# A state scan on VectorE: one multiplication of 1024 columns in place of two of 512

## The reference

```python
# d_inner 256 = 2 halves of 128, d_state 16, L 256, batch 4
def step(state, inp):
    d, b, c, u = inp
    dA = jnp.exp(d[..., None] * A)
    state = state * dA + (d * u)[..., None] * b[:, None, :]
    y = jnp.einsum('bdn,bn->bd', state, c)
    return (state, y)
_, ys = jax.lax.scan(step, state0, (dt_t, B_t, C_t, u_t))
y = ys + D * x;  y = y * silu(z)
```

## Time and profile before

| | |
|---|---|
| median of 3 runs | 593.02 us (589.87 to 594.47) |
| profiled execution, its own time | 595.68 us |
| its span | 593.4 us |
| TensorE matmul busy | 483.5 us, 81% |
| VectorE busy | 472.9 us, 80% |
| ScalarE busy | 363.0 us, 61% |
| GpSimd busy | 280.7 us, 47% |
| mean granted TensorE clock | 0.930 |

### The profile page before, as it was taken

The page is one execution under the profiler, slowest core; times in us unless marked ns, Lnnn a source line. Parts: engine busy times, 40 slices in busy tenths (PEclk is TensorE's granted clock), DMA queues, the critical chain, the costliest instruction groups (busy, mean ns, idle before and its releaser), DMA issues.

```text
span 593.4 us, 10199 instructions
## 1 busy us (share of the span) xinstructions
PE 483.5 (81%) x3040; PEld 360.9 (61%) x3050; DVE 472.9 (80%) x1246; ACT 363.0 (61%) x830; POOL 280.7 (47%) x262
## 2 busy tenths in 40 slices
PE   6817777767778879898989999998799988998823
PEld 3302222222357757576779899997689977997602
DVE  4899999999875537897666765896898969875886
ACT  2785555536227745464767676678665796778543
POOL 3119777879210444561068548732786234333111
PEclk9957999989869989899999999999999999999856
DMA  5939300001003589998242103400135000000000
GB/s 157 224 72 335 97 0 1 1 1 35 1 9 114 193 235 290 282 284 236 83 159 64 28 8 73 64 2 2 36 56 72 1 2 2 19 2 0 1 18 18
DMA packets 45624, 48.60 MB, mean 82 GB/s; under 512 B 5660, under 2 KB 42118, under 8 KB 45574
## 3 DMA queue, kind: packets, MB, share of 16 engines
q1 hardware_dynamic: 41734, 36.46, 22.6%
q0 software_dynamic: 3840, 11.54, 8.6%
HBM read 41.43 MB, written 6.56 MB: 81 GB/s over the span
## 4 chain that ended last, share of the span: by engine, by line
PE 33%; DVE 26%; issue 22%; ACT 8%; POOL 8%; DMA 1%; DVEq 1%; SPq 0%; POOLq 0%; ACTq 0%; another core or an unknown queue 0%
DVE hst L1786 7%; PE ps L1539 5%; PE ps L1478 4%; PE ps L1479 4%; PE ps L1480 4%; PE ps L1528 3%; PE ps L1395 2%; POOL dbu L524 2%; DVE hc L1795 2%; POOL G L603 2%; POOL pn L619 2%; PE ps L1292 1%; PE ps L1432 1%; PE ps L1196 1%; PE ps L1380 1%
## 5 line engine op out<-in xcount | busy, mean ns | idle before, releaser
L619 POOL TENSOR_TENSOR pn<-pr,pinv 128x512 f32<-128x512 f32 x64 | 67.6, 1059 | 88.3 <-DVE pinv L2194 87.9
L524 POOL TENSOR_TENSOR dbu<-du,brow 128x512 f32<-128x512 f32 x64 | 81.5, 1285 | 41.4 <-DVE du L1779 23.1
L1196 PE MATMUL ps<-hc,ident 128*128 128x512 f32 x128 | 75.7, 683 | 28.9 <-DVE hc L1795 27.4
L1786 DVE TENSOR_TENSOR_SCAN hst<-ps,dbu 128x512 f32<-128x512 f32 x64 | 77.4, 1210 | 0.2 <-POOL dbu L524 0.2
L762 ACT ACTIVATE ps<-dtv,amat 128x510 f32<-128x510 f32 x64 | 44.1, 690 | 50.9 <-DVE hst L1786 50.1
L938 ACT ACTIVATE pr<-ebuf,smin 128x256 f32<-128x256 f32 x128 | 63.7, 502 | 13.0 <-DVE smin L2185 6.6
L1539 PE MATMUL ps<-pT,cS 128*128 128x256 f32 x256 | 67.2, 385 | 0.0
L581 POOL DMA_INDIRECT G<-token_rows,idx_x x32 | 39.9, 1246 | 52.1 <-DVE ebuf L2039 24.0
L1196 PEld LDWEIGHTS ps<-hc,ident 128*128 128x128 f32 x128 | 21.0, 202 | 69.6 <-DVE hc L1795 66.9
L603 POOL DMA_INDIRECT G<-expert_out,idx_g x48 | 51.1, 1064 | 11.6 <-issue 10.4
L2185 DVE CUSTOM_DVE_ANT_0 ebuf<-ps,mbias 128x256 f32<-128x256 f32 x128 | 48.9, 419 | 6.2 <-issue 6.0
(11 more groups left out here) (372 smaller groups left out, 1364.8 us busy)
## 6 DMA issues: line engine op xcount, KB each, us to landing
wdn<-in_L_ffn_wd SPq DMA_DIRECT2D x15, 384.0 KB
wgu<-in_L_ffn_wg SPq DMA_DIRECT2D x14, 384.0 KB
wgu<-in_L_ffn_wu SPq DMA_DIRECT2D x14, 384.0 KB
expert_out<-xn SPq DMA_DIRECT2D x11, 256.0 KB
wq<-in_L_xattn_Wq SPq DMA_DIRECT2D x2, 1024.0 KB, 9.2
wo<-in_L_xattn_Wo SPq DMA_DIRECT2D x1, 2048.0 KB, 15.6
wo<-in_L_ffn_w SPq DMA_DIRECT2D x2, 1024.0 KB, 6.9
expert_out<-pexp SPq DMA_DIRECT2D x5, 256.0 KB
```

Source lines behind the costliest of these rows:

```text
L524: nc.gpsimd.tensor_tensor(dbu[:, j, :], du[:, j % 2, 512 * hb:512 * hb + 512], brow[:, j // 2, :], ALU.mult).then_inc(pool_dbu, 1)
L619: nc.gpsimd.tensor_tensor(pn[:, h % 2], pr[:, h % 2], pinv[:, h % 2, :].unsqueeze(2).to_broadcast([P, 2, L]), ALU.mult)\
L1196: pe.matmul(bank(2 + j % 2), ident[:], hc[:, j % 2, :], start=(isinstance(m, int) and m + k == 0), stop=(isinstance(m, int) and m + k == N ...
L1786: V.tensor_tensor_scan(hst[:, j, :], bank(j % 2), dbu[:, j, :], 0.0, ALU.mult, ALU.add)\
```

## The change

VectorE multiplies the states of both inner halves by their C row in one operation of 1024 columns, with the bank of the row broadcast over the halves. The product buffer now holds two pairs: `hc` is one, the tile `wqT`, which isn't in use yet, the other. `hc_ready` counts pairs. A pair's product is taken after both its scans, so the order for four is scan 0, pair 1 of the last group, scan 1, scan 2, pair 0, scan 3. TensorE waits once for a pair and then makes both additions. Before `sum_up(0)`, `add_scan` and `lower_logits` the last product in VectorE's order is now a pair; ahead of `sum_up(1)` the pair with both halves comes behind `choose(0)` and `shares(0)`.

```diff
+        products = (hc[:], wqT[:].rearrange("p a b l -> p a (b l)"))
...
-                for j in (2 * k, 2 * k + 1):
-                    i = 32 * hb + 4 * m + j
-                    pe.wait_ge(hc_ready, i + 1)
-                    pe.matmul(bank(2 + j % 2), ident[:], hc[:, j % 2, :], start=(isinstance(m, int) and m + k == 0),
+                pe.wait_ge(hc_ready, 16 * hb + 2 * m + k + 1)
+                for d in range(2):
+                    pe.matmul(bank(2 + d), ident[:], products[k][:, d, :], start=(isinstance(m, int) and m + k == 0),
                               stop=(isinstance(m, int) and m + k == NS // 2)).then_inc(y_added, 1)
...
-                wait_count(dve, hc_ready, i - 3)
+                wait_count(dve, hc_ready, 16 * hb + 2 * m + j // 2 - 1)
...
-            def read_out(hb, m, j):
+            def read_out(hb, m, k):
 
-                i = 32 * hb + 4 * m + j
-                dve.wait_ge(scanned, i + 1)
-                dve.wait_ge(c_spread, 16 * hb + 2 * m + j // 2 + 1)
-                wait_count(dve, y_added, i - 1)
-                V.tensor_tensor(hc[:, j % 2, :], hst[:, j, :], bank(6 + j // 2), ALU.mult).then_inc(hc_ready, 1)
+                i = 32 * hb + 4 * m + 2 * k
+                dve.wait_ge(scanned, i + 2)
+                dve.wait_ge(c_spread, 16 * hb + 2 * m + k + 1)
+                wait_count(dve, y_added, i - 2)
+                V.tensor_tensor(products[k], hst[:, 2 * k:2 * k + 2, :],
+                                bank(6 + k).unsqueeze(1).to_broadcast([P, 2, 512]), ALU.mult).then_inc(hc_ready, 1)
 
             def scan_four(hb, m, first):
-                for j in range(4):
-                    scan(hb, m, j)
-                    if j:
-                        read_out(hb, m, j - 1)
-                    elif not first:
-                        read_out(hb, m - 1, 3)
+                scan(hb, m, 0)
+                if not first:
+                    read_out(hb, m - 1, 1)
+                scan(hb, m, 1)
+                scan(hb, m, 2)
+                read_out(hb, m, 0)
+                scan(hb, m, 3)
...
-                for j in (2 * k, 2 * k + 1):
-                    scan(1, m, j)
-                    if j:
-                        read_out(1, m, j - 1)
-                    elif m:
-                        read_out(1, m - 1, 3)
-                    else:
-                        read_out(0, NS // 2 - 1, 3)
+                scan(1, m, 2 * k)
+                if k:
+                    read_out(1, m, 0)
+                elif m:
+                    read_out(1, m - 1, 1)
+                else:
+                    read_out(0, NS // 2 - 1, 1)
+                scan(1, m, 2 * k + 1)
                 if n == 0:
                     sum_up(0)
...
-            read_out(1, NS // 2 - 1, 3)
+            read_out(1, NS // 2 - 1, 1)
             sum_up(1)
```

## The result

The changed kernel takes 599.69 us (median of 6 runs, 598.64 to 602.26) against 591.15 us for the kernel before on the same chips (6 runs, 589.86 to 594.47). The ratio is 1.014, 95% interval 1.011 to 1.017: slower by 8.5 us. The profiled execution took 599.31 us with a span of 597.0. The one before took 595.68 us, more than any of its six other runs, so these two alone would say +3.6 us. Comparisons inside the scan stage are therefore made between the traces, and those of the whole kernel between the medians. What lies behind the stage can't be compared between single traces: that part of the program is the same in all nine, and from the last L1810 or its counterpart to the end of the span it took between 419.8 and 428.1 us.

The account below looks back on a forecast made before the run. The prediction took VectorE to bound the scan stage. Its terms, -1.4 + 4.6 + 1.1 + 1.6 + 1.3 = +7.2 us, carried whole onto the median of 593.02 us, gave 600.2 us, with a range of 593.5 to 605.

Parts of the forecast that it names:

- The saving: Steady scan stage: a long product's slot of 1.12 us replaces 1.16, 0.045 us a pair, -1.4 us over 31 pairs.
- both doubts: Steady scan stage: successive scans might not overlap, +2.6 us; the PSUM broadcast might cost 0.04 us an operation, leaving no saving.
- L1820 twice and L1839: Turned outputs and logits of half 0: each existing VectorE wait for TensorE grows by 1.54 us, +4.6 us.
- L1812 after the first half: First half's sums: later products cost 1.54 us less 0.44 us of cover, a wait of +1.1 us.
- The end of the stage: Last sums: the path from last multiplication becomes 4.86 us with TensorE at 1.2 GHz, +1.6 us; at 2.4 GHz +0.2.
- The start: First scans: a decay behind a B row copy behind a late spread, +1.2 us, and the third scan's decay, +0.1.
- Carried whole: Behind the scan stage: nothing swallows the delay, so all +7.2 us reach the kernel's time.
- grouping simply pays: Rival, whole kernel: late products hidden or swallowed, only the saving left, 589 to 592 us; chance 0.06 for 587 to 592.
- the third: Rival, scan stage: long product no faster than two short, -1.4 us lost, 601.6 us; inside the forecast's range, no separate chance.
- The clock rival: Second L1818: TensorE at 1.2 GHz after idling, +2.0 us; with non-overlapping scans 602 to 605 us; clock or scans chance 0.15.

Follow-up runs that it names:

- The order alone: Changed kernel with its order kept, but each pair multiplied in two operations of 512 columns that signal separately; 595.38 us, ratio 1.0064 to the kernel before.
- the late rows: Changed kernel with ScalarE's copy of a B row put one decay later in its queue; 595.75 us, ratio 1.0077 to the kernel before.
- TensorE kept busy: Changed kernel with 14 and 17 matmuls that nobody reads added at two places where TensorE sat idle; 599.77 us, ratio 1.0128 to the kernel before.
- the kernel before with a delay: Kernel before plus six chained, unread VectorE operations of 1024 columns ahead of the scan stage's last product; 599.48 us, ratio 1.0129.
- the kernel with halves: Changed kernel with the nine of 32 pairs next to a wait multiplied in single halves, in the earlier order; 589.72 us, ratio 0.9985 to the kernel before.
- the waits further on and the B rows late: Changed kernel with readers of TensorE's results one step later, B row copies one decay later, last pair in halves; 590.07 us, ratio 0.9938 to the kernel before.

## Why the prediction was right

Slower, at 600.2 us forecast and 599.69 measured, and for the reason given: products arrive later at places where VectorE then waits. That the two times lie 0.5 us apart is luck. The forecast added 7.2 us to a median of 593.02 from three runs; with six runs the kernel before has 591.15, and the growth is 8.5 us (6.5 to 10.0 by the interval). The firmer comparison is the stage: in the profiled executions it grew by 7.0 us, where 7.2 were forecast. By the prediction's own steps:

- **The saving.** Forecast -1.4 us; measured 31 x 0.065 = -2.0. The pitch of four scans fell from 6.85 to 6.72 us where 6.75 was forecast: the long product's slot is 1.11, not 1.12, and two scans on end have a pitch of 1.12. Scans overlap on end and the broadcast of a PSUM bank costs nothing over the copy in SBUF; both doubts fell on the good side. By the figure for PSUM of the Trainium skill ("Perfetto Trace Analysis", Optimizing Scalar/DVE Operations), 125 ns, it would have been an estimated 4.0 us. A removed operation gave 0.065 us here, about half of that; the same sentence of the Trainium skill has about 60 ns for SBUF, and these operations read one operand from each.
- **L1820 twice and L1839.** Forecast +4.6 us, with waits of 2.0, 2.0 and 3.0; measured 1.8, 1.8 and 2.9, so +4.2. The longer product was sized right (0.54 us), the second addition a little too high: the forecast took 0.96 us from the earlier trace rows, the distance from the start of the first addition to that of the spread, and the second one adds 0.87. The order alone showed the two parts apart.
- **L1812 after the first half.** Forecast +1.1; measured a wait of 0.94 us where there was none:

```profile
101.80 1.98 PE L1196 MATMUL ps<-wqT,ident 128*128 128x512 f32 x4 [0.94 <-DVE wqT L1795]
...
103.82 1.40 DVE L1812 SCALAR_TENSOR_TENSOR u<-u,dskip,ps 128x512 f32<-128x512 f32 x2 [0.94 <-PE ps L1196]
```

- **The end of the stage.** This term was mis-sized: +1.6 us forecast at 1.2 GHz, +0.1 measured. The timeline and the stretch (length, busy PE, PEld, DVE, ACT, POOL, granted clock, DMA share, GB/s) show 1.00 where the earlier trace rows had 0.50:

```profile
170.88 1.21 DVE L1795 TENSOR_TENSOR wqT<-hst,ps 128x1024 f32<-128x1024 f32 x1
...
172.14 1.98 PE L1196 MATMUL ps<-wqT,ident 128*128 128x512 f32 x4 [1.16 <-DVE wqT L1795]
...
174.17 1.41 DVE L1812 SCALAR_TENSOR_TENSOR u<-u,dskip,ps 128x512 f32<-128x512 f32 x2 [2.08 <-PE ps L1196]
```

```profile
172.00:174.00 2.00, 1.86 (x6) 0.81 (x7) 0.09 (x1) 0.00 (x0) 0.00 (x0) 1.00 0.22 57
```

  The path is 3.29 us; the prediction had 3.39 for 2.4 GHz and 4.86 for 1.2, and took the second because "TensorE is no busier ahead of it than before". That premise failed. The late pairs kept TensorE at work until 1.16 us before these additions, against 1.99 us in the earlier trace rows. The clock wasn't kept up throughout, though: it had fallen behind the logits and had only just come back:

```profile
164.03 3.78 PE L1196 MATMUL ps<-wqT,ident 128*128 128x512 f32 x4 [3.22 <-DVE wqT L1795]
```

```profile
168.00:170.00 2.00, 1.98 (x3) 0.94 (x3) 1.93 (x14) 0.00 (x0) 0.00 (x0) 0.50 0.00 0
170.00:172.00 2.00, 0.99 (x2) 0.07 (x1) 1.93 (x5) 0.00 (x0) 0.00 (x0) 0.95 0.04 9
```

  Before, it was 0.50 from 160 to 162 us, 0.98 in the next two and 0.50 again at the last additions. So both kernels had a fall after the logits and a return; a second fall came only before. Whether the length of the idle time decides that was not tried.
- **The start.** Forecast +1.2 for a scan that waits for ScalarE and +0.1 for the third scan; measured 1.42 and 0.0:

```profile
54.52 0.60 ACT L771 ACTIVATE brow<-ps 128x512 f32<-128x512 f32 x1 [2.74 <-PE ps L1179]
...
55.73 1.22 DVE L1786 TENSOR_TENSOR_SCAN hst<-ps,dbu 128x512 f32<-128x512 f32 x1 [1.42 <-ACT ps L763]
```

  The copy waits for the spread and the decay behind the copy, as worked out; the late rows took the wait away.
- **Not in the sum.** Two more waits for ScalarE, 0.39 us at 112.35 and 1.20 us at 137.69, each behind a fall of the clock (0.50 from 110 to 112 us, after TensorE had idled 3.40 us, and 0.50 from 130 to 136):

```profile
132.06 3.78 PE L1196 MATMUL ps<-wqT,ident 128*128 128x512 f32 x4 [5.17 <-DVE wqT L1795]
...
136.48 0.60 ACT L771 ACTIVATE brow<-ps 128x512 f32<-128x512 f32 x1 [2.62 <-PE ps L1179]
...
137.69 1.22 DVE L1786 TENSOR_TENSOR_SCAN hst<-ps,dbu 128x512 f32<-128x512 f32 x1 [1.20 <-ACT ps L763]
```

  TensorE idles 5.17 us behind the waits, its additions then take 3.78 us instead of 1.98, the spread behind them is late, and ScalarE's copy and decay with it. The prediction had named the new idle time after L1810 and after the first L1818, but priced the clock only at the second L1818; there it fell in one of the traces. The path on which a slow TensorE reaches VectorE, through ScalarE's queue, it had worked out for the start of the stage alone. TensorE kept busy removes the two, and so do the late rows. By size this omission (+1.6) made up for the end of the stage (-1.5); that the total came so close is luck in that part.

Measured, the terms are -2.0 + 4.2 + 0.9 + 0.1 + 1.4 + 1.6 = +6.2 us; the first scan started 0.1 us later, and four waits that are new each cost the 0.08 us by which neighbours otherwise overlap, +0.3. 0.4 us of the 7.0 stay unassigned.

**Carried whole.** The forecast's last step is supported by the kernel before with a delay (7.5 us in, 7.5 out). In the two traces alone it could be doubted: the first expert product comes 5.4 us later and the end 3.6. But from the last sums to the end the trace before has 426.2 us, the changed one 422.8, and the kernel with halves, which ends its stage earlier than either, 421.8. So that part varies by itself and doesn't follow the stage's end, and the medians differ by 8.5.

**The rivals.** That grouping simply pays is refuted for this placing; with the waits further on and the B rows late it holds, for 1.8 us. The long product is faster than two short ones, so the third is refuted. The clock rival is real, but in the changed kernel's profile it cost 1.6 us at other places than the one named.

The Trainium skill ("Perfetto Trace Analysis", Optimizing Scalar/DVE Operations) also says that where ScalarE or VectorE isn't saturated but makes others wait, breaking an instruction up may let work end sooner. Here VectorE is the saturated engine, and breaking up nine pairs of 32, in the order of before, still gave about 9 us back (ratio 0.9985 instead of 1.014), because VectorE itself waited for the reader of its own products.

## What to carry to other kernels

Before operations of the busiest engine are grouped, list the places where that engine waits for a result that stands in another's queue behind its products: at each, the grouped form costs its longer duration plus the consumer's extra operation (here 0.54 + 0.87 us), and a handful of such places outweigh 31 savings of 0.065 us. Group where nothing waits, keep the small form beside the waits, or move the waits one step down first; then the same grouping paid here, with the copies in ScalarE's queue moved as well. Look in the same way behind the first engine's new idle time: the copy and decay in ScalarE's queue behind a late spread became waits of VectorE that no single row of before showed.

## What was not expected of the hardware

TensorE's granted clock fell to 0.50 in stretches that came at different places in kernels with nearly the same program: in or just behind idle times of 3.40, 5.17 and 3.22 us, around 108, 129 and 163 us, in the changed kernel, and in one of 3.09 us before 122 us with the rows late, but not in one of 3.08 us before 124 us in the changed kernel. It nearly doubled the additions' time where it fell (1.98 to 3.78 us), and with matmuls in two of the gaps it stayed at 1.00 from 100 to 160 us, over a gap of 3.09 us at 123 us that was left open. At the end of the stage the same additions met 0.50 before and 1.00 after. What decides between these was not settled.
